# A four-layer graph network on one core: one self-loop edge of each node taken out of the edge tiles

## What is computed

```python
src = jnp.concatenate([_s, _d, _loop]); dst = jnp.concatenate([_d, _s, _loop])
_o = jnp.argsort(dst, stable=True); src, dst = src[_o], dst[_o]
...
x = _layernorm(x + _L0(x, deg ** -0.5, src, dst))      # 10 hops: h = 0.9*norm*segment_sum((h*norm)[src], dst) + 0.1*h0
x = _layernorm(x + _L1(x, [src, dst], ...))            # two attention layers of 4 heads (GAT), then a linear map
x = _layernorm(x + _L2(x, [src, dst], type, weight))   # out[dst] += (x @ W[type])[src] * weight, over 8 relations
x = _layernorm(x + _L3(x, src, dst, ...))              # 8-head attention exp(clip(K[src].Q[dst])), batch norm, MLP
# in each attention layer of _L1 the loops are appended once more:
src = jnp.concatenate([edge_index[0], loop]); dst = jnp.concatenate([edge_index[1], loop])
```

## Time and profile before

| | us |
|---|---|
| median of 3 runs (3444.05 to 3447.16) | 3445.85 |
| the profiled execution | 3445.47 |
| its span, first to last instruction | 3443.4 |
| POOL busy / DVE busy / PE busy / ACT busy | 1916.2 / 2090.3 / 2161.0 / 1240.0 |
| indirect DMAs of the four passes, POOL | 1760 |

### The profile page before, as it was taken

One profiled execution on the slowest core, in us unless ns is written; L12 is line 12 of the kernel. 1 busy time (PEld: TensorE's weight loads), 2 busy tenths in 40 slices (PEclk: granted clock), 3 DMA queues, 4 the chain that ended last, 5 costly groups with the idle time before them and its releaser, 6 DMA issues.

```text
span 3443.4 us, 43202 instructions
## 1 busy us (share of the span) xinstructions
PE 2161.0 (63%) x14597; PEld 1879.9 (55%) x14598; DVE 2090.3 (61%) x5511; ACT 1240.0 (36%) x1290; POOL 1916.2 (56%) x1899
## 2 busy tenths in 40 slices
PE   4887999999994555556356666633333334544455
PEld 3557999999993444445244444422333324444454
DVE  8996766666683666667467676723333225555555
ACT  4886666666662233222223333200000012222222
POOL 2222222222224777776577777467777767777770
PEclk9998999999997777777677777766666666666667
DMA  2000000000005444443445555422222224444441
GB/s 57 20 1 0 0 0 0 0 0 0 0 0 174 130 141 134 139 141 104 131 133 153 159 159 155 118 63 59 59 58 59 59 78 133 129 129 133 132 119 35
DMA packets 139378, 283.85 MB, mean 82 GB/s; under 512 B 35751, under 2 KB 79123, under 8 KB 139155
## 3 DMA queue, kind: packets, MB, share of 16 engines
q0 software_dynamic: 77760, 204.68, 21.8%
q1 hardware_dynamic: 24603, 53.25, 4.7%
q10 hardware_dynamic: 36864, 24.07, 2.3%
HBM read 255.10 MB, written 27.01 MB: 82 GB/s over the span
## 4 chain that ended last, share of the span: by engine, by line
POOL 42%; issue 14%; PE 6%; DVE 5%; DMA 2%; ACT 1%; ACTq 0%; POOLq 0%; DVEq 0%
POOL t_rows L1945 19%; POOL t_rows L2314 11%; POOL t_rows L2643 11%; PE t_sum_ps L2045 2%; PE t_product_ps L1714 1%; DVE t_rows L2127 1%; PE t_sum_ps L2335 1%; DMA t_rows<-gat_table,t_src 1%; PE t_sum_ps L2694 0%; DMA t_rows<-rel_table_b,t_rel 0%; DMA t_rows<-kv_table_b,t_src 0%; DVE t_onehot L1873 0%; PE t_small_ps L2499 0%; PE t_product_ps L2507 0%; PE t_small_ps L2015 0%
## 5 line engine op out<-in xcount | busy, mean ns | idle before, releaser
L1945 POOL DMA_INDIRECT t_rows<-gat_table,t_src x880 | 837.1, 951 | 322.8 <-issue 265.6
L1063 PE MATMUL hop_ps<-parts,wide 128*128 128x256 f32 x5900 | 713.1, 283 | 5.3 <-DVE parts L1158 4.1
L1063 PEld LDWEIGHTS hop_ps<-parts,wide 128*128 128x128 f32 x5900 | 709.9, 192 | 7.8 <-issue 4.2
L1114 ACT CAST wide<-counts 128x3200 fp32r<-128x3200 fp8e4 x177 | 506.3, 2863 | 232.3 <-PE hop_ps L1063 212.0
L2045 PE MATMUL t_sum_ps<-t_rows,t_onehot 128*128 128x264 f32 x1760 | 488.8, 445 | 100.7 <-DVE t_rows L2127 100.7
L2314 POOL DMA_INDIRECT t_rows<-rel_table_b,t_rel x440 | 417.7, 949 | 179.0 <-issue 132.0
L2643 POOL DMA_INDIRECT t_rows<-kv_table_b,t_src x440 | 418.0, 950 | 148.9 <-issue 132.2
L1123 POOL CAST wide<-counts 128x3200 fp32r<-128x3200 fp8e4 x59 | 168.7, 2859 | 589.6 <-PE hop_ps L1063 565.1
L2045 PEld LDWEIGHTS t_sum_ps<-t_rows,t_onehot 128*128 128x128 f32 x1760 | 389.4, 225 | 183.6 <-issue 103.8
L2335 PE MATMUL t_sum_ps<-t_rows,t_onehot 128*128 128x128 f32 x880 | 157.5, 362 | 330.5 <-DMA t_rows<-rel_table_b,t_rel 330.5
L2335 PEld LDWEIGHTS t_sum_ps<-t_rows,t_onehot 128*128 128x128 f32 x880 | 153.2, 275 | 338.1 <-issue 335.2
(11 more groups left out here) (373 smaller groups left out, 3320.3 us busy)
## 6 DMA issues: line engine op xcount, KB each, us to landing
t_dst_wide<-dst_row SPq DMA_DIRECT2D x72, 576.0 KB, 4.2
t_rows<-gat_table,t_src POOLq DMA_INDIRECT x880
rel_table_b<-t_stage ACTq DMA_DIRECT2D x25, 512.0 KB, 3.7
t_rows<-rel_table_b,t_rel POOLq DMA_INDIRECT x440, 2.5
t_rows<-kv_table_b,t_src POOLq DMA_INDIRECT x440, 2.8
gat_table<-t_own ACTq DMA_DIRECT2D x10, 520.0 KB, 4.7
kv_table_b<-t_fresh ACTq DMA_DIRECT2D x5, 512.0 KB, 3.0
out<-x SPq DMA_DIRECT2D x6, 256.0 KB
```

The costliest lines, as they stand in the source:

```text
L1063: last = nc.tensor.matmul(ps[bank][0:columns.shape[-1], 0:2 * D], columns[:, k, :], parts[old][:, k, :], start=(k == 0), stop=(k == NB - 1))
L1114: nc.scalar.copy(wide[b % B][:, :, :], column(b)).then_inc(widened, 1)
L1945: c.nc.gpsimd.indirect_dma_start(t.rows[:, slot(k), 0:FW], None, self.table, bass.IndirectOffsetOnAxis(ap=t.src[:, k:k + 1], axis=0)).then ...
```

## The change

`CAP` goes from 18 to 17 and `CAP_TAIL` from 8 to 7: 415 tiles in place of 440. One loop edge of each node, found as a self-edge at the end of its node's run, is left out of the tiles and put back at the node:

- **Ordering.** DVE marks the loop edges that go (`gone`), counts them by a running sum (`before`), and closes the gaps by six rounds of a conditional shift by 1, 2, 4, 8, 16 and 32 places: a bit test of `KEEP` (L341) into PSUM and a predicated copy of all four fields (L342). Each chunk has a halo of 64 edges, so the columns are 480. Type, source and target of an edge are packed into one `CODE` (three POOL additions, from ACT products), since `KEEP` and `NEXT` (the type and weight of the loop behind the edge) take their places; they are unpacked after the gather. The rows go to HBM by two indirect DMAs of POOL, one after the other.
- **Counting.** Degrees are handled in four lots. For each lot PE ranks nodes, DVE locates each node's last edge, POOL gathers its row (`fetch_own`, 25 indirect DMAs), and DVE adds the loop to the diagonal of `counts`. PE's first transposes now also wait for `consts` = 4, which POOL signals behind its start-up constants.
- **GAT passes.** The node's own weight gets `bias` = ln 2 where a loop was taken out.
- **Relations.** `mix` adds `x @ W[r]` of the node's own loop by eight chained DVE operations a block, blocks 0 to 19 in the second GAT pass and 20 to 24 in the relations pass. The ring `t.stage` grows to 6 blocks.
- **Cross.** ACT keeps V of each node, DVE makes K.Q of the loop, and both join the sums in `close`.

```diff
-CAP = 18
-CAP_TAIL = 8
+CAP = 17
+CAP_TAIL = 7
+SHIFTS = [1 << k for k in range(6)]
...
+                then(v.tensor_tensor(loop[:, :], src_i[:, :], dst_i[:, :], ALU.is_equal))
+                then(v.scalar_tensor_tensor(gone[:, 1:W - 1], change[:, 0:W - 2], 0.0, loop[:, 1:W - 1], ALU.is_equal, ALU.mult))
+                then(v.tensor_tensor(gone[:, 1:W - 1], gone[:, 1:W - 1], change[:, 1:W - 1], ALU.mult))
+                then(v.tensor_tensor_scan(before[:, :], gone[:, :], gone[:, :], 0.0, ALU.add, ALU.max))
...
+                for shift in SHIFTS:
+                    reach -= shift
+                    n = max(reach, CH)
+                    then(v.tensor_scalar(moves[:, 0:n], keep[:, shift:shift + n], shift, None, ALU.bitwise_and))
+                    then(v.copy_predicated(rows[:, 0:n, :], moves[:, 0:n].rearrange("p (j o) -> p j o", o=1).to_broadcast([P, n, NF]), rows[:, shift:shift + n, :]))
+                dve.nop().then_inc(closed, 1)
...
+                for odd in range(2):
+                    p.indirect_dma_start(chunks, bass.IndirectOffsetOnAxis(ap=chunk_to[:, odd:odd + 1], axis=1),
+                                         rows[odd * 64:(odd + 1) * 64, 0:CH, :].rearrange("p j f -> p (j f)"), None).then_inc(written, 16)
+                    pool.wait_ge(written, 16 * (odd + 1))
...
+                then(v.tensor_copy(code_i[:, :, :], field(c.by_slot, CODE)))
+                v.tensor_scalar(type_i[:, :, :], code_i[:, :, :], 19, None, ALU.arith_shift_right)
+                then(v.tensor_scalar(high_i[:, :, :], code_i[:, :, :], 7, None, ALU.arith_shift_right))
+                v.scalar_tensor_tensor(rel, type_i[:, :, :], float(NP - 4096), high_i[:, :, :], ALU.mult, ALU.add)
+                v.scalar_tensor_tensor(src, type_i[:, :, :], -4096.0, high_i[:, :, :], ALU.mult, ALU.add)
+                then(v.scalar_tensor_tensor(dst, high_i[:, :, :], -float(P), code_i[:, :, :], ALU.mult, ALU.add))
...
+LOTS = [range(0, 7), range(7, 15), range(15, 22), range(22, NB)]
+LOT_AT = {blocks[-1] + 2: i for i, blocks in enumerate(LOTS[:-1])}
...
+                def fetch_own(i):
+                    pool.wait_ge(located, i + 1)
+                    for b in LOTS[i]:
+                        nc.gpsimd.indirect_dma_start(c.own_rows[:, b, :], None, c.edges,
+                                                     bass.IndirectOffsetOnAxis(ap=last_at[:, b:b + 1], axis=0)).then_inc(own_landed[i], 16)
...
+                pe.wait_ge(consts, 4)
                 for n, f in enumerate((SRC, DST, REL, WGT)):
...
+                def own_edges(i):
+                    lo, hi = LOTS[i][0], LOTS[i][-1] + 1
+                    dve.wait_ge(own_landed[i], 16 * len(LOTS[i]))
...
+                    for b in LOTS[i]:
+                        at = counts[:, b, b * P:b * P + width(b)]
+                        last = v.scalar_tensor_tensor(at, c.ident[:, 0:width(b)], c.own_has[:, b:b + 1], at, ALU.mult, ALU.add, saturate=False)
+                    then(last)
                 for b in range(NB):
+                    if b in LOT_AT:
+                        degrees_of(LOT_AT[b])
                     for n, k in enumerate(tiles_of(b)):
+                        if b in LOT_AT and n == HALF:
+                            locate(LOT_AT[b])
+                            if LOT_AT[b]:
+                                own_edges(LOT_AT[b] - 1)
...
+    def mix(self, dve, b):
+        c, t, v = self.c, self.t, self.c.nc.vector
+        then = chained(dve, self.mix_step, b * NREL)
+        total = t.own[:, b, 0:D]
+        for r in range(NREL):
+            last = v.scalar_tensor_tensor(total, t.stage[:, b % STAGES, r * D:(r + 1) * D], t.own_rel[:, r, b:b + 1], total, ALU.mult, ALU.add)
+            then(last)
+        dve.nop().then_inc(self.mixed, 1)
...
+            for _, blocks in LATE.get(b - 1, []):
+                self.after.dve_mix(dve, blocks)
+        for _, blocks in LATE.get(NB - 3, []):
+            self.after.dve_mix(dve, blocks)
         x, y, z = NB - 3, NB - 2, NB - 1
```

## The result

The changed kernel takes 3415.84 us (median of 4 runs, 3412.60 to 3417.38) beside 3444.95 for the kernel before; the ratio is 0.9913, 95% interval 0.9896 to 0.9931. It is faster by 29 us, where 62 were forecast, and it lies 5.8 us above the upper end of the range. The profiled execution took 3412.60 us, its span is 3410.5.

What follows compares the result with a forecast made beforehand. POOL's gather beat of 1.25 us bounds the four passes, DVE ordering and counting, PE the hops. 29 + 17 - 30.1 - 16.8 - 31.2 - 30.8 + 0.5 = -62.4 from 3445.5: 3383 us, range 3362 to 3410.

Steps and rivals of the forecast that it cites:

- The hops don't change.: Between counting and the first GAT gather: no change claimed, with only +0.5 us in the sum for the blocks' start.
- Copies under a mask: Ordering, closing the gaps: six predicated copies of 11016 elements at 1.22 ns each, 13.4 us, bounds 8.5 and 22.8.
- Rival 3: Ordering: closing eats the gain; predicated copies from 6.9 ns an element make it slower, 3458 us at 8 ns; 4%.
- Bit tests: Ordering: six bit tests over 2754 elements a partition at 1.19 ns each, 3.3 us, priced by L331's same stride.
- DVE's wait for the packing: Ordering: DVE waits 2.7 us, between 0 and 7, behind POOL's three packing additions, taken at 1 us each.
- Unpacking: Ordering, behind the gather: one strided conversion, two shifts and three strided operations, +5.0 us.
- Transposes: Start of counting: PE's transposes wait for POOL's last constants and delay DVE's start, +5.4 us.
- Counting's blocks: Counting: one tile less a block -9.3 us, three degree waits +5.1, last lot exposed at the end +8.2.
- First GAT pass: First GAT pass: block 22's last tile lands 23 tiles earlier, 28.8 us, and the tail shortens; -30.1 us.
- Second GAT pass: Second GAT pass: -16.8 us; 21 tiles earlier -26.2, mixes in the last iterations +10.4, DVE just keeping POOL's beat.
- Cross: Cross pass: 25 tiles fewer at POOL's 1.25 us beat, -30.8 us, with +0.5 at the very end.
- Rival 2: Counting: each of 25 own-row gathers holds up a DVE comparison 0.95 us and is itself held up, 3407 us; 11%.

Runs made afterwards that it cites:

- The experiment: Changed kernel with PE's wait for POOL's start-up constants moved from ahead of counting's transposes to the ranking; 3870.88 us on the slower chip.
- the second profile: The changed kernel itself, unaltered, run again on another chip: 3414.25 us beside 3445.99 for the kernel before, ratio 0.9908.
- the kernels with later fetches: Changed kernel with counting's degree copies, ranking and locating later in the block, so later fetches: 3410.67 us; also combined with other edits, 3365.14 and 3363.68.
- the kernel with free transposes: Changed kernel with PE's wait for POOL's constants put at the ranking, not ahead of counting's transposes; 3870.88 us on the slower chip.

## Why the prediction was wrong

**The step that failed** is four words at the end of the counting part, "The hops don't change.", and a sum that has nothing but +0.5 us between them and the first gather. The hops don't change, but the stores of the first GAT table behind them do. I read `CAP` as a number of tiles, and counted what 17 tiles save. It is also a number of partitions. The loads of the cut windows were outside the diff and their tile appears in the earlier trace rows as 72 partitions; I listed what the change adds and removes, and not what else `CAP` shapes. +25.4 us for +0.5, and 27.5 to 29 us back when the load is split. With it the sum would have been 3383 + 25 = 3408. None of the rivals had a transfer that changes its shape.

**The rest of the sum** is 4.7 us off in the profiled execution (29.6 - 24.9), and some of that closeness is luck: ordering, counting, the second GAT pass and relations are 9.8 us over, the first GAT pass and cross 5.1 under, 4.0 of these in a tail that the sum did not work out. With the loads split the kernel takes 3386.7, where 3383 was forecast. Step by step:

- *Copies under a mask.* 13.2 us for 11016 elements, 1.20 ns each, forecast 13.4 at 1.22. Rival 3, from 6.9 ns on, is dead.
- *Bit tests.* 5.8 us for a forecast of 3.3. The row that I took as the price, L331 in the earlier trace rows, has the stride but not the destination; the mask lay in PSUM.
- *DVE's wait for the packing.* 4.25 for 2.7, since POOL's additions take 1.86, 1.49 and 1.21 us and not 1 each. Loads 1.8 us later, not 0.5, and marking 0.8 longer. The comparison starts at 39.14 instead of 33.2.
- *Unpacking.* +4.4 by its rows for +5.0.
- *Transposes.* First `hot_src` later by 38.93 us, of which 33.57 are ordering: +5.4, as forecast. The experiment says that 4.15 of it can be had back.
- *Counting's blocks.* Most plain blocks take 7.98 to 8.07 us, as the prediction asked, and four 8.5 to 8.7. Degree waits are 1.44, 1.44 and 2.61 us (1.44 three times in the second profile), forecast 1.5 each. From DVE's last digits to the hops it is 15.1 us for 6.6 before, +8.5 for +8.2. Left over are +5.1 for tiles and lots where +3.4 was forecast.
- *First GAT pass* -31.2 for -30.1, *relations* -30.4 for -31.2: close to 25 tiles at 1.25 us, which are 31.25.
- *Second GAT pass.* -14.5 for -16.8. `raise_(22)` to `raise_(23)` takes 35.47 us, forecast near 34; the 32 mixes take 12.70, forecast 12.5. A cycle of four iterations takes 85.3 to 85.9 us, forecast 85.0, against 85.3 to 85.6 without mixes, and POOL's beat is unbroken. The account was right and the gain 2.3 us too large.
- *Cross.* -34.8 for -30.8. The tail behind the last gather is 4.6 us shorter: DVE's wait of 1.68 us for the last landing is gone, and so is its wait of 1.76 for PE's sums of the last block. That this comes of 7 tiles at the end and not 8 is likely but not tested. I had the tail at +0.5.

**Rival 2** (fetches against comparisons) is nearly dead. The 25 fetches take 28.4 us, 1.14 each for the gathers' 0.95, up to 1.93 (2.28 in the kernels with later fetches). Seven comparisons beside them take 2.57 to 2.58 us, what they take alone. What the fetches cost is POOL's time: the unpackings stand behind them. In the Trainium skill, "SBUF — State Buffer", section "SBUF: two separate sides", a DMA of POOL took about 3100 ns beside a fast DVE copy. Nothing near it is seen here. The prediction's rows could not decide it, either: the comparisons of the passes, which it set against the rule, are 32-bit ones with an operand in PSUM, and the rule speaks of certain fast forms; no run shows whether they are among them.

The lock that the same section describes, one of the two engines waiting for the whole instruction of the other, does fit the rows where POOL computes. DVE's 0.39 us beside `iota_s` becomes 1.54 and ends 0.26 behind it; its 0.64 beside a packing addition becomes 1.46. In the counting stage of the changed kernel 225 comparisons with no POOL instruction beside them take 0.43 us each, 47 beside a fetch 0.44, and 62 beside one of POOL's unpackings 0.69 on average, up to 0.84. The kernel before has the same (0.43 and 0.70 for 292 and 70). So these operations of DVE are held up by POOL's computing instructions and not by its DMAs, which are themselves 0.19 us longer on average. Not every operation is: `hot_src` takes 0.80 to 0.81 us in either company.

## What to carry to other kernels

When a constant that counts tiles changes, look up every transfer whose partitions or rows it sets, not only the loops that it shortens: 18 to 17 partitions cost 25 us here, in four loads that the diff does not contain. A transfer confined to one DMA engine is not only slow itself (36 us where 7 had been enough); it holds up the full-width transfers of other queues, and the engine that issues them. And a row gives the price of an operation only if stride, type and destination are the same, PSUM or SBUF among them. Moving DVE's work into a time when POOL computes can give back a good part of what the move wins, here 2.0 of 6.2 us and 1.7 of 4.2.

## What the runs showed of the hardware

- Four loads of 17 partitions, 12850 bytes in each, go packet by packet on one DMA engine: 68 packets in 36 us, where 72 of 18 partitions took 6.9. Beside the stores of another queue the engine alternates, one packet of each. The rate is then 19 to 37 GB/s, where the queues otherwise move 300 to 390, and the issue of a store on the other queue took 9.5 and 14.6 us in place of 0.37.
- A predicated copy of 32-bit words, the mask broadcast over four, costs 1.19 to 1.23 ns an element, whether the mask is in PSUM or SBUF. A bitwise operation on 478 elements that reads int32 with a stride of four words costs 1.21 ns an element into SBUF and 2.09 into PSUM.
- A 16-bit comparison of DVE takes 0.43 us alone or beside a DMA of POOL, and 0.69 on average beside one of POOL's conversions (62 of them).
- One chip took 3921 us for the kernel that others run in 3445. POOL's gathers were 0.96 us there too, against 0.95. But DVE stopped for up to 22 us in 1200 to 1650 us of the kernel with free transposes on that chip, and the group with the largest sum has `remote` as its releaser, none of the core's engines or DMAs (sum, times, longest):

```profile
DVE t_own_l L2300 <- remote: 56.6, 5, 21.2
```

In the changed kernel on the chip of the result the longest wait of DVE in that stretch is 6.8 us. What stopped the engines stays open.
